# First attention: the high and low parts of Q and K made from PSUM by one ScalarE and one VectorE instruction, and copied to their rows by DMA

## The chip, the cores and the metric

The kernel runs on one core of a Trainium2 chip. The metric is the device time in microseconds of one execution; before the change it is 2598.87 us (median of three runs).

## The reference

The kernel computes one block of a hybrid network on x of 2048 x 128 in fp32:

```
x = x + attn_a(layernorm(x))   # 16 heads of 64, biases, a scale per head, softmax over all 2048 keys,
                               # output projection, residual and a layernorm inside
x = x + ffn(layernorm(x))      # 128 -> 512 -> 128, relu
x = x + attn_b(layernorm(x))   # 8 heads of 128, rotary embedding, causal
x = x + ffn(layernorm(x))

attn_a:  Q = x Wq' + bq,  K = x Wk' + bk,  V = x Wv' + bv
         scores = Q K' * (64 ** -0.5 * adaptive_scale[head]);  softmax;  times V;  times Wo
```

Only the first attention (attn_a) is touched.

## The kernel before, in words

**Precision by parts.** A score needs more precision than one fast product gives. So each operand is split into a high part (rounded to the fp32r format) and a low part (what the rounding left). For a head, four arrays of 128 rows hold Q and K, transposed, with 2048 columns: KH has K-high in both halves of its rows, QL has Q-low in one half and Q-high in the other, QH has Q-high in its upper half (and the rows of maxima in its first rows), KL has K-low there. A score tile is then two products of 128 rows each: KH by QL (L1297) and KL by QH (L1298). There are two sets of the four arrays, for the head in work and the next.

**Pattern.** A unit is one head and one block of 512 queries; a head has four units, a loop turn of the program two heads, so eight units, here numbered 0 to 7. A unit has eight steps of 256 keys. In a step TensorE makes four score products (L1297, L1298) and, with a lag of two steps, sixteen products of probabilities by V (L1247, L1248). ScalarE takes two exponentials of the scores, 128 x 1024 each, to fp32 (L634) and to fp16 (L636). GpSimd subtracts one from the other to get the low part of the probabilities (L449). All engines are programmed apart and meet by semaphores.

**The ring.** Everything else that TensorE does for later units goes through two PSUM banks used in turn, RING: a product is put into one, VectorE takes it out, in order, and the counter `ring_taken` says so. `ring_items_a` writes the order out by hand: sixteen rough score tiles, from which VectorE takes maxima (L855), spread over steps 0 to 6 of a unit; in units 5, 6, 7 and 0 "turned" in step 3 and "output" in step 4 (the output projection of the pair of heads); in steps 3 and 7 of units 0, 1, 4 and 5 one projection each, which makes a block of 512 columns of Q and K for the next head (L1173); in units 2 and 6 the values; and last in step 7 "rows", the transposed maxima (L858 to L860, L1200, L867), which VectorE writes into QH. At step 0 of a unit TensorE waits until all items of the ring are taken.

**A projected block.** VectorE adds the bias and multiplies by the scale, from PSUM into F (L824), Q in rows 0 to 63 and K in rows 64 to 127. ScalarE then copies it in five pieces of 64 rows, rounded, to KH, QL, KH, QL and QH (L594); `PIECES` spreads these over the four steps that follow, one or two in each behind the step's exponentials. Two steps later VectorE subtracts for K-low (L831), GpSimd for Q-low (L426). The first maximum of a head waits for all of it. SP's queue issues only the loads of weights ahead of the attention and what follows it.

In the head of the program the weights are transposed by TensorE and taken from PSUM by ScalarE and VectorE in turn; the four blocks of head 0 are projected there one after another. VectorE does the statistics of each finished unit in step 2 of the next (L888 to L892).

Of the kernel before, what the change touches and what calls it, by code (L numbers as in the profile page):

```python
# [41 lines left out]
P = 128  # L42
# [19 lines left out]
PIECES = ((0, 1), (2,), (3,), (4,))  # L62

WV_AT = 2 * DA + 2
# [121 lines left out]
def build(nc, x, adaptive_scale, Wq, bq, Wk, bk, Wv, bv, Wo, bo, gamma, beta,  # L186
          w_aq, w_ak, w_av, w_ao, W1, b1, W2, b2, rope_cos, rope_sin, out):
    ctx = ExitStack()
    with ctx:
# [18 lines left out]
        F = sb("F", [P, 2, BLK])  # L208
        WST = sb("WST", [P, 2, 3 * DB])
        OSUM = sb("OSUM", [P, 2, BT // 2, DA])  # L210
# [38 lines left out]
        sraw = F[0:DA, 1, P:P + HA]  # L249
# [52 lines left out]
        k_low = sem("k_low")  # L302
# [45 lines left out]
        def _(sp):  # L348
# [7 lines left out]
            sp.dma_start(sraw, adaptive_scale.partition_broadcast(DA)).then_inc(w_in, 16)  # L356
# [14 lines left out]
            sp.dma_start(WVB, w_av).then_inc(bweights, 16)  # L371

# [12 lines left out]
        def _(pool):  # L385
# [31 lines left out]
            pool.wait_ge(wt_act, 5)  # L417
# [34 lines left out]
            for blk in range(BLOCKS):  # L452
                q_low(0, blk, blk)
# [12 lines left out]
            def turn_a(it, first=False, last=False):  # L466
                for ul in range(UNITS_A):
# [5 lines left out]
                    for step in range(STEPS_A):  # L473
                        two, three = (after_a(ul, step, d, first, last) for d in (2, 3))
                        if two and two[0] == "project":
                            q_low(1 - hs, two[1], head * BLOCKS + two[1])
                        elif two:
                            values_rest(1 - hs, two[1], head * 2 + two[1])
# [72 lines left out]
        def _(act):  # L551
# [17 lines left out]
            for i in range(0, 9, 2):  # L569
# [3 lines left out]
                if i < 4:  # L573
                    ins = act.activation(WQK[:, i * 4:i * 4 + 4, 0:P], src4, ACT.Copy)
                elif i < 6:
                    ins = act.activation(WQK[:, 0:8, WV_AT:BV_AT], bank.rearrange("p (a c) -> p a c", c=DA), ACT.Copy)
                elif i < 8:
                    ins = act.activation(WoT[:, (i - 6) * 4:(i - 6) * 4 + 4, :], src4, ACT.Copy)
                else:
                    ins = act.activation(WQK[:, :, P], bank[:, 0:HA], ACT.Copy)  # L580
                ins.then_inc(wt_act, 1)
# [26 lines left out]
            for blk in range(BLOCKS):  # L608
                high_parts_a(0, blk, blk, 0, range(5))
# [15 lines left out]
            def exps_a(it, first=False, last=False):  # L625
                k = SKIP if first else 0
                numbers = {}
                for ul in range(UNITS_A):
                    hs, qb = divmod(ul, BLOCKS)
                    for step in range(STEPS_A):  # L630
# [8 lines left out]
                        for delay, pieces in enumerate(PIECES, 1):  # L639
                            item = after_a(ul, step, delay, first, last)  # L640
                            if item and item[0] == "project":
                                high_parts_a(1 - hs, item[1], LEAD_A - SKIP + it * RING_A + numbers[item],
                                             (head - 1) * BLOCKS * STEPS_A, pieces)
                            elif item and delay == 1:
                                values_first(1 - hs, item[1], LEAD_A - SKIP + it * RING_A + numbers[item])
                            elif item and delay == 2:
                                values_second(1 - hs, item[1], head * 2 + item[1])
                        for item in ring_items_a(ul, step, first, last):
                            numbers[item] = k
                            k += 1  # L650
# [105 lines left out]
        def _(dve):  # L756
# [45 lines left out]
            for i in range(1, 8, 2):  # L802
                dve.wait_ge(wt_put, i + 1)
                bank = QUARTER[i % 4]
                src4 = bank.rearrange("p (a c) -> p a c", c=P)
                if i < 4:
                    ins = dve.tensor_copy(WQK[:, i * 4:i * 4 + 4, 0:P], src4)
                elif i < 6:
                    ins = dve.tensor_copy(WQK[:, 8:HA, WV_AT:BV_AT], bank.rearrange("p (a c) -> p a c", c=DA))
                else:  # L810
                    ins = dve.tensor_copy(WoT[:, (i - 6) * 4:(i - 6) * 4 + 4, :], src4)
                ins.then_inc(wt_dve, 1)
            dve.wait_ge(w_in, 80)

            dve.memset(WQK[DA:P, :, P + 1], 1.0)
            dve.tensor_scalar(WQK[0:DA, :, P + 1], sraw, SCALE_A, None, ALU.mult).then_inc(wt_dve, 1)
# [745 lines left out]
```

## Time and profile before

| | |
|---|---|
| three runs, us | 2598.98, 2596.69, 2598.87 |
| median | 2598.87 |
| profiled execution, first to last instruction (its span) | 2594.6 |
| its TensorE clock, mean granted share | 0.975 |
| busy, share of the span | TensorE 92%, VectorE 68%, ScalarE 67%, GpSimd 57% |
| first attention, first to last score product of its loop | 54.7 to about 1720 us |

A share of busy time is a mean over the whole program. Of the execution with the profile the page gives only the span; the runs' own times are those of the first line, and the part outside the span is the difference of the two.

### The profile page before, as it was taken

To read this page: it belongs to the slowest core of one execution; us is meant where nothing else is said; L and a number is where in the kernel's file an instruction comes from. 1 tells how busy PE (TensorE), PEld (TensorE's weight loads), DVE (VectorE), ACT (ScalarE), POOL (GpSimd) and SP (SyncE) were. 2 spreads that over 40 slices of the span, in tenths; PEclk is the share of its full clock that TensorE was granted. 3 is DMA by queue.
4 is the path that set the end of the run, shared out by engine and by line. 5 is a ranking of instruction groups with operands and counts; after the bars stand their busy time and mean duration, and the time that the engine had idled before them with its cause. 6 is when DMAs were issued, how large, how long until landed. Compare 5 with 4: busy or idle time off the path is not lost.

```text
span 2594.6 us, 47816 instructions
## 1 busy us (share of the span) xinstructions
PE 2390.6 (92%) x17315; PEld 1882.8 (73%) x17315; DVE 1769.3 (68%) x3012; ACT 1732.4 (67%) x2190; POOL 1469.7 (57%) x826
## 2 busy tenths in 40 slices
PE   5999999999899899989989999977899999999998
PEld 3777777677777677767767777754788887888786
DVE  6777767677677677767776777666666665666652
ACT  4877877778688687777878878752455454455554
POOL 5787777677687677767777777753122112122200
PEclk7999999999999999999999999988899999999999
DMA  3000000000000000000000000010000000000000
GB/s 94 1 1 1 1 1 1 2 1 1 2 1 1 2 1 1 2 2 1 1 2 1 1 1 1 1 41 1 1 1 1 1 1 2 1 1 1 1 1 17
DMA packets 15276, 13.06 MB, mean 5 GB/s; under 512 B 3120, under 2 KB 14384, under 8 KB 14768
## 3 DMA queue, kind: packets, MB, share of 16 engines
q1 hardware_dynamic: 15024, 9.72, 1.4%
q8 instruction: 156, 2.56, 0.4%
q14 instruction: 96, 0.79, 0.1%
HBM read 8.67 MB, written 1.05 MB: 4 GB/s over the span
## 4 chain that ended last, share of the span: by engine, by line
PE 46%; issue 26%; DVE 13%; POOL 9%; ACT 4%; SPq 0%; DMA 0%; DVEq 0%; POOLq 0%; ACTq 0%
PE OO L1247 6%; PE RING L1193 6%; PE ST L1297 5%; POOL PAB L449 5%; PE ST L1298 5%; DVE maxes L855 4%; PE OO L1248 4%; PE OO L1436 3%; DVE OSUM L889 2%; PE RING L1214 2%; POOL F L512 2%; PE RING L1173 2%; PE RING L1389 1%; PE ST L1459 1%; ACT PAB L636 1%
## 5 line engine op out<-in xcount | busy, mean ns | idle before, releaser
L449 POOL TENSOR_TENSOR PAB<-PR,PAB 128x1024 f16<-128x1024 f32 x512 | 1093.2, 2137 | 407.8 <-ACT PAB L636 390.1
L855 DVE TENSOR_REDUCE maxes<-RING 128x1 f32<-128x512 f32 (+1 forms) x1344 | 883.9, 670 | 417.4 <-PE RING L1193 294.1
L634 ACT ACTIVATE PR<-ST,lift 128x1024 f32<-128x1024 f32 x512 | 569.1, 1111 | 360.0 <-PE ST L1298 354.0
L1247 PE MATMUL OO<-VP,PAB 128*128 128x194 bf16 x4096 | 688.3, 250 | 5.5 <-POOL PAB L449 2.0
L1248 PE MATMUL OO<-VP,PAB 128*128 128x130 bf16 x4096 | 653.3, 220 | 0.0
L636 ACT ACTIVATE PAB<-ST,lift 128x1024 f16<-128x1024 f32 x512 | 565.8, 1105 | 0.0
L1247 PEld LDWEIGHTS OO<-VP,PAB 128*128 128x128 f16 x4096 | 400.7, 98 | 190.4 <-issue 127.1
L1193 PE MATMUL RING<-KH,QL 128*128 128x512 f32 x1024 | 457.0, 453 | 46.4 <-DVE maxes L855 39.7
L1297 PE MATMUL ST<-QL,KH 128*128 128x512 f32 x1024 | 453.9, 443 | 29.2 <-issue 13.7
L1248 PEld LDWEIGHTS OO<-VP,PAB 128*128 128x128 f16 x4096 | 403.7, 99 | 10.8 <-issue 9.9
L1298 PE MATMUL ST<-QH,KL 128*128 128x512 f32 x1024 | 405.6, 396 | 0.0
L512 POOL TENSOR_TENSOR F<-F,PR 128x512 f32<-128x512 f32 x64 | 81.4, 1272 | 508.9 <-DVE PR L1023 508.9
L719 ACT ACTIVATE PR<-ST 128x512 f32<-128x512 f32 (+1 forms) x320 | 169.4, 529 | 260.5 <-PE ST L1463 258.5
L1193 PEld LDWEIGHTS RING<-KH,QL 128*128 128x128 f32 x1024 | 196.1, 192 | 139.0 <-DVE maxes L855 117.8
L1436 PEld LDWEIGHTS OO<-PAB,PR 128*128 128x128 f32 x1536 | 227.4, 192 | 41.1 <-issue 22.7
L1436 PE MATMUL OO<-PAB,PR 128*128 128x129 f32 x1536 | 250.7, 280 | 0.0
L1297 PEld LDWEIGHTS ST<-QL,KH 128*128 128x128 f32 x1024 | 195.5, 191 | 66.4 <-issue 38.7
L1298 PEld LDWEIGHTS ST<-QH,KL 128*128 128x128 f32 x1024 | 195.9, 191 | 33.0 <-issue 7.2
L700 ACT ACTIVATE ST<-VF 128x512 f32<-128x512 f32 (+1 forms) x320 | 172.0, 538 | 26.7 <-PE ST L1425 15.3
L1459 PE MATMUL ST<-QH,KH 128*128 128x512 f32 (+1 forms) x320 | 146.3, 457 | 1.0
L1389 PE MATMUL RING<-KH,QH 128*128 128x512 f32 (+2 forms) x320 | 129.3, 408 | 14.7 <-ACT PR L719 8.1
L831 DVE TENSOR_TENSOR KL<-F,KH 64x512 fp32r<-64x512 f32 x64 | 120.5, 1882 | 24.5 <-ACT KH L594 24.0
(132 smaller groups left out, 3044.4 us busy)
## 6 DMA issues: line engine op xcount, KB each, us to landing
X<-in_L_attn_a_x SPq DMA_DIRECT2D x4, 256.0 KB, 4.3
SHARED<-in_rope_cos SPq DMA_DIRECT2D x1, 1024.0 KB, 4.9
SHARED<-in_rope_sin SPq DMA_DIRECT2D x1, 1024.0 KB, 7.1
out<-X SPq DMA_DIRECT2D x4, 256.0 KB, 2.3
RAW<-in_L_attn_a_Wq SPq DMA_DIRECT2D x1, 512.0 KB, 7.5
RAW<-in_L_attn_a_Wk SPq DMA_DIRECT2D x1, 512.0 KB, 7.8
RAW<-in_L_attn_a_Wv SPq DMA_DIRECT2D x1, 512.0 KB, 5.7
RAW<-in_L_attn_a_Wo SPq DMA_DIRECT2D x1, 512.0 KB, 6.8
```

What stands on the lines that cost most here:

```text
L449: pool.tensor_tensor(PB[:, s, :], PR[:, step % 2, :], PA[:, s, :], ALU.subtract).then_inc(p_low_pool, 1)
L634: act.activation(PR[:, step % 2, :], ST[step % 2][:, :], ACT.Exp, bias=lift[:, :])
L636: act.activation(PA[:, step % SLOTS_A, :], ST[step % 2][:, :], ACT.Exp, bias=lift[:, :]).then_inc(sa.exps, 1)
L700: act.activation(SB[parity][:, c0:BLK], MB[:, slot, c0:BLK], ACT.Copy).then_inc(sbb.filled, 1)
L855: dve.reduce_max(maxes[:, qt, c:c + 1], bank[:, 0:width], X_AXIS).then_inc(s.ring_taken, 1)
L1193: pe.matmul(bank[:, :], QL[hs][:, at:at + P], KH[hs][:, c * BLK:(c + 1) * BLK], start=True, stop=True).then_inc(sa.ring_put, 1)
L1247: pe.matmul(o, high, v, start=(m == 0 and qt % 2 == 0), stop=False, skip_group_check=True)
L1248: ins = pe.matmul(o[:, 0:V3_AT], low, v[:, 0:V3_AT], start=False, stop=(m == TILES - 1), skip_group_check=True)
L1297: pe.matmul(tile, KH[hs][:, keys], QL[hs][:, q], start=True, stop=False)
L1298: ins = pe.matmul(tile, KL[hs][:, keys], QH[hs][:, q], start=False, stop=True)
L1436: ins = pe.matmul(bank[:, at:at + VB], PRB[:, step % 2, qt * P:(qt + 1) * P], VBS[:, ul // BLOCKS, step, :], start=(step == 0 and qt in (0 ...
L1459: pe.matmul(tile, KH[hs][:, keys], QH[hs][:, q], start=False, stop=False, skip_group_check=True)
```

## The change

The scale is multiplied into the weights and the bias of Q once, in the head of the program. A projected block is then read from PSUM twice: by ScalarE, which adds the bias and rounds, into a new buffer HS (the high parts of Q and K), and by VectorE, which adds the bias and subtracts HS, into F (the low parts). Both use all 128 rows. ScalarE's instruction stands in the step of the projection, behind its exponentials. The bank counts as taken when VectorE is done. SP waits for that and issues six DMAs of 64 rows x 512, which put the parts in their rows of KH, QL, QH and KL. The five pieces, K-low and Q-low go. HS and F are written again only when the moves of two blocks earlier have landed. The weights of Q and K are now all taken from PSUM by VectorE, with the scale; those of V and of the output by ScalarE. The staged weights are one column narrower.

```diff
-PIECES = ((0, 1), (2,), (3,), (4,))
+MOVES = 6
-WV_AT = 2 * DA + 2
+WV_AT = 2 * DA + 1
...
+            def move_parts(hs, blk, item, scores_before):
+
+                sp.wait_ge(sa.ring_taken, item + 1)
+                wait(sp, sa.scores, scores_before)
+                q = slice(blk * BLK, (blk + 1) * BLK)
+                high, low = HS[:, blk % 2, :], F[:, blk % 2, :]
+                for dst, src in ((KH[hs][0:DA, q], high[DA:P, :]), (KH[hs][DA:P, q], high[DA:P, :]),
+                                 (QL[hs][0:DA, q], high[0:DA, :]), (QL[hs][DA:P, q], low[0:DA, :]),
+                                 (QH[hs][DA:P, q], high[0:DA, :]), (KL[hs][DA:P, q], low[DA:P, :])):
+                    sp.dma_start(dst.bitcast(F32), src).then_inc(parts_moved[blk % 2], 16)
...
-            def q_low(hs, blk, index):
-
-                pool.wait_ge(sa.high_ready, index * 5 + 2)
-                at = QL[hs][0:DA, blk * BLK:(blk + 1) * BLK]
-                pool.tensor_tensor(at, F[0:DA, blk % 2, :], at.bitcast(F32), ALU.subtract
-                                   ).then_inc(sa.operands_ready, 1)
...
-            def high_parts_a(hs, blk, item, scores_before, pieces):
-
-                act.wait_ge(sa.ring_taken, item + 1)
-                wait(act, sa.scores, scores_before)
-                q = slice(blk * BLK, (blk + 1) * BLK)
-                f = F[:, blk % 2, :]
-                places = ((KH[hs], DA, DA), (QL[hs], 0, 0), (KH[hs], 0, DA), (QL[hs], DA, 0), (QH[hs], DA, 0))
-                for i in pieces:
-                    dst, to, at = places[i]
-                    act.activation(dst[to:to + DA, q], f[at:at + DA, :], ACT.Copy).then_inc(sa.high_ready, 1)
+            def high_parts_a(hs, blk, bank, item, batch):
+
+                act.wait_ge(sa.ring_put, item + 1)
+                wait(act, parts_moved[blk % 2], batch * MOVES * 16)
+                act.activation(HS[:, blk % 2, :].bitcast(F32R), bank[:, :], ACT.Identity,
+                               bias=WST[:, hs, P:P + 1]).then_inc(sa.high_ready, 1)
...
                         for item in ring_items_a(ul, step, first, last):
+                            if item[0] == "project":
+                                high_parts_a(1 - hs, item[1], RING[(LEAD_A - SKIP + k) % 2],
+                                             LEAD_A - SKIP + it * RING_A + k, head * (BLOCKS // 2) + item[1] // 2)
                             numbers[item] = k
                             k += 1
...
-            def take_projected_a(hs, blk, bank, item, index):
-
-                dve.wait_ge(sa.ring_put, item + 1)
-                wait(dve, sa.operands_ready, index - 1)
-                wait(dve, sa.high_ready, (index - 1) * 5)
-                wait(dve, k_low, index - 1)
-                dve.tensor_scalar(F[:, blk % 2, :], bank[:, :], WST[:, hs, P:P + 1],
-                                  WST[:, hs, P + 1:P + 2], ALU.add, ALU.mult).then_inc(sa.ring_taken, 1)
-
-            def take_k_low(hs, blk, index):
-
-                dve.wait_ge(sa.high_ready, index * 5 + 1)
-                q = slice(blk * BLK, (blk + 1) * BLK)
-                dve.tensor_tensor(KL[hs][DA:P, q], F[DA:P, blk % 2, :], KH[hs][DA:P, q].bitcast(F32),
-                                  ALU.subtract).then_inc(k_low, 1)
+            def take_projected_a(hs, blk, bank, item, index, batch):
+
+                dve.wait_ge(sa.high_ready, index + 1)
+                wait(dve, parts_moved[blk % 2], batch * MOVES * 16)
+                dve.scalar_tensor_tensor(F[:, blk % 2, :].bitcast(F32R), bank[:, :], WST[:, hs, P:P + 1],
+                                         HS[:, blk % 2, :], ALU.add, ALU.subtract).then_inc(sa.ring_taken, 1)
...
             def max_a(hs, qb, i, bank, item, head):
                 if i == 0 and qb == 0:
-                    pe.wait_ge(sa.operands_ready, (head + 1) * BLOCKS)
-                    pe.wait_ge(k_low, (head + 1) * BLOCKS)
-                    pe.wait_ge(sa.high_ready, (head + 1) * BLOCKS * 5)
+                    for moved in parts_moved:
+                        pe.wait_ge(moved, (head + 1) * (BLOCKS // 2) * MOVES * 16)
```

## Rows read from the trace of the kernel before

**Rows 1.** The page, part 1: busy us, share, instructions of each engine.

```profile
PE 2390.6 (92%) x17315; PEld 1882.8 (73%) x17315; DVE 1769.3 (68%) x3012; ACT 1732.4 (67%) x2190; POOL 1469.7 (57%) x826
```

**Rows 2.** Windows of units 0, 1, 4, 5, two without projection, and steps 3 to 4.

```profile
core 0: us, PE busy (x) PEld busy (x) DVE busy (x) ACT busy (x) POOL busy (x), PEclk, DMA share, GB/s
258.06:283.96 25.90, 24.85 (x196) 19.04 (x194) 19.20 (x30) 20.51 (x22) 19.70 (x11) 1.00 0.01 2
283.96:309.78 25.82, 24.48 (x182) 17.67 (x182) 19.73 (x29) 23.04 (x27) 20.39 (x10) 1.00 0.01 2
360.42:385.29 24.87, 23.58 (x184) 17.68 (x182) 18.37 (x28) 19.33 (x20) 18.34 (x10) 1.00 0.01 2
385.29:412.03 26.74, 25.71 (x193) 19.02 (x194) 20.48 (x31) 23.09 (x27) 20.39 (x10) 1.00 0.00 1
1633.02:1654.64 21.62, 21.48 (x180) 16.94 (x178) 14.90 (x25) 16.95 (x18) 17.09 (x9) 1.00 0.00 1
1654.64:1678.03 23.39, 22.79 (x192) 18.14 (x190) 16.29 (x27) 16.95 (x18) 17.12 (x9) 1.00 0.01 2
368.50:375.71 7.21, 6.66 (x50) 4.68 (x48) 5.73 (x9) 4.31 (x5) 4.61 (x3) 1.00 0.00 0
1641.12:1647.06 5.94, 5.80 (x49) 4.38 (x46) 4.96 (x8) 4.31 (x5) 4.63 (x3) 1.00 0.01 3
```

**Rows 3.** Timeline, steps 5 and 6 of the unit at 360.42: start, us.

```profile
376.43 0.63 ACT L594 ACTIVATE KH<-F 64x512 fp32r<-64x512 f32 x1
...
377.09 2.08 DVE L831 TENSOR_TENSOR KL<-F,KH 64x512 fp32r<-64x512 f32 x1 [1.03 <-ACT KH L594]
...
379.95 0.50 PE L1193 MATMUL RING<-KH,QL 128*128 128x512 f32 x1 [0.41 <-DVE maxes L855]
```

**Rows 4.** Groups by line: busy us, mean ns, idle before.

```profile
L831 DVE TENSOR_TENSOR KL<-F,KH 64x512 fp32r<-64x512 f32 x64 | 120.5, 1882 | 24.5 <-ACT KH L594 24.0
...
L892 DVE TENSOR_TENSOR SHARED<-OSUM,rden 128x256 f32<-128x256 f32 x64 | 96.8, 1513 | 2.2
```

**Rows 5.** Groups by line, the operations nearest to the new ones.

```profile
L878 DVE TENSOR_TENSOR XN<-XN,RING 128x512 f32<-128x512 f32 x32 | 22.0, 687 | 28.2 <-PE RING L1214 28.2
...
L663 ACT ACTIVATE PAB<-ST,b1c 128x512 f32<-128x512 f32 x16 | 10.7, 693 | 9.0 <-PE ST L1332 8.8
```

**Rows 6.** Timeline, GpSimd and VectorE in step 7 of unit 3.

```profile
357.02 2.13 POOL L449 TENSOR_TENSOR PAB<-PR,PAB 128x1024 f16<-128x1024 f32 x1 [0.51 <-ACT PAB L636]
...
357.05 2.11 DVE L860 TENSOR_TENSOR negparts<-negmax,negparts 128x4 f32<-128x4 f32 x1
```

**Rows 7.** Timeline of unit 4: step 0's exponential, then step 7.

```profile
361.63 1.12 ACT L634 ACTIVATE PR<-ST,lift 128x1024 f32<-128x1024 f32 x1 [2.03 <-PE ST L1298]
...
381.70 0.47 PE L1297 MATMUL ST<-QL,KH 128*128 128x512 f32 x1
...
383.18 1.11 ACT L634 ACTIVATE PR<-ST,lift 128x1024 f32<-128x1024 f32 x1
...
383.77 0.81 DVE L824 TENSOR_SCALAR F<-RING,WST 128x512 f32<-128x512 f32 x1 [1.12 <-PE RING L1173]
...
384.19 1.11 ACT L636 ACTIVATE PAB<-ST,lift 128x1024 f16<-128x1024 f32 x1
...
384.50 0.67 DVE L867 TENSOR_TENSOR QH<-RING,rowmask 8x512 fp32r<-8x512 f32 x1
```

**Rows 8.** DMA issues of the page: count, KB each, us to landing.

```profile
out<-X SPq DMA_DIRECT2D x4, 256.0 KB, 2.3
```

**Rows 9.** Timeline of the prologue: first maximum's product, GpSimd's last addition.

```profile
37.68 1.19 PE L1193 MATMUL RING<-KH,QL 128*128 128x512 f32 x2 [1.77 <-ACT QH L594]
...
48.53 4.49 POOL L463 TENSOR_TENSOR X<-X,beta_b 128x2048 f32<-128x2048 f32 x1
```

**Rows 10.** Windows: a held subtraction (unit 3), then the turn of the loop.

```profile
355.00:359.30 4.30, 2.52 (x23) 1.85 (x21) 3.83 (x5) 3.76 (x4) 3.63 (x2) 1.00 0.00 0
...
465.60:469.10 3.50, 1.00 (x15) 0.80 (x12) 0.60 (x1) 0.00 (x0) 2.46 (x2) 0.99 0.03 9
469.10:472.50 3.40, 3.34 (x14) 2.50 (x14) 0.69 (x1) 1.23 (x2) 0.00 (x0) 0.50 0.03 7
```

More of the change, by code:

```diff
@@ L301, in build @@
         ones_set = sem("ones_set")
-        k_low = sem("k_low")
+        parts_moved = [sem(f"parts_moved{i}") for i in range(2)]
         p_low_pool = sem("p_low_pool")
@@ L371, in _, with moves_a @@
             sp.dma_start(WVB, w_av).then_inc(bweights, 16)
+            def move_parts(hs, blk, item, scores_before):
[7 more added lines that the diff above has]
+                    sp.dma_start(dst.bitcast(F32), src).then_inc(parts_moved[blk % 2], 16)
+            def moves_a(it, first=False, last=False):
+                k = SKIP if first else 0
+                for ul in range(UNITS_A):
+                    hs = ul // BLOCKS
+                    head = it * 2 + hs + 1
+                    for step in range(STEPS_A):
+                        for item in ring_items_a(ul, step, first, last):
+                            if item[0] == "project":
+                                move_parts(1 - hs, item[1], LEAD_A - SKIP + it * RING_A + k,
+                                           (head - 1) * BLOCKS * STEPS_A)
+                            k += 1
+            for blk in range(BLOCKS):
+                move_parts(0, blk, blk, 0)
+            moves_a(0, first=True)
+            with sp.Fori(1, ITER_A - 1) as it:
+                moves_a(it)
+            moves_a(ITER_A - 1, last=True)
             wait(sp, sa.ring_taken, END_A)
@@ L474, in turn_a @@
                         two, three = (after_a(ul, step, d, first, last) for d in (2, 3))
-                        if two and two[0] == "project":
-                            q_low(1 - hs, two[1], head * BLOCKS + two[1])
-                        elif two:
+                        if two and two[0] == "values":
                             values_rest(1 - hs, two[1], head * 2 + two[1])
@@ L568, in _ @@
                 deviations(b)
-            for i in range(0, 9, 2):
+            for i in range(4, 8):
                 act.wait_ge(wt_put, i + 1)
@@ L638, in exps_a @@
                         head = it * 2 + hs + 1
-                        for delay, pieces in enumerate(PIECES, 1):
+                        for delay in (1, 2):
                             item = after_a(ul, step, delay, first, last)
[L641 to L644, printed above, removed]
+                            if item and item[0] == "values" and delay == 1:
                                 values_first(1 - hs, item[1], LEAD_A - SKIP + it * RING_A + numbers[item])
-                            elif item and delay == 2:
+                            elif item and item[0] == "values":
                                 values_second(1 - hs, item[1], head * 2 + item[1])
                         for item in ring_items_a(ul, step, first, last):
+                            if item[0] == "project":
+                                high_parts_a(1 - hs, item[1], RING[(LEAD_A - SKIP + k) % 2],
+                                             LEAD_A - SKIP + it * RING_A + k, head * (BLOCKS // 2) + item[1] // 2)
                             numbers[item] = k
@@ L801, in _ @@
             dve.tensor_copy(later_keys_t[:, :], mask_raw[:, 1, :]).then_inc(const_r, 1)
-            for i in range(1, 8, 2):
+            dve.memset(score_scale[:, :, 1], 1.0)
+            dve.wait_ge(w_in, 80)
+            link(dve.tensor_scalar(score_scale[:, :, 0], sraw, SCALE_A, None, ALU.mult))
+            for i in range(4):
                 dve.wait_ge(wt_put, i + 1)
[L804 to L812, printed above, removed]
@@ L921, in body_a @@
                             normalise_a((ul - 1) % UNITS_A, u)
-                        two = after_a(ul, step, 2, first, last)
-                        if two and two[0] == "project":
-                            take_k_low(1 - hs, two[1], index + two[1])
                         late = (step - 1) % STEPS_A in LOW_BY_DVE and not (first and ul == 0 and step == 0)
@@ L1149, in _ @@
                     pe.wait_ge(vw_in, 48)
[L1150 to L1151 removed]
+                if 4 <= i < 8:
+                    pe.wait_ge(wt_dve, i - 3)
+                elif i == 8:
+                    pe.wait_ge(wt_act, 1)
                 bank = QUARTER[i % 4]
```

46 lines of the change are left out of this document (22 added, 24 removed).

## The prediction

> **What bounds the kernel now.** I read the page first: TensorE is busy 92% of the span, VectorE, ScalarE and GpSimd between 57 and 68% [rows 1]. So TensorE sets the pace and work taken from another engine is worth only the TensorE waits that it causes. These can't be read from busy shares. The first attention repeats one pattern, so next I cut it into units (one head's block of 512 queries, eight steps) and compared their lengths in the windows view, each from the first score matmul of a unit (L1297) to that of the next [rows 2]. The reader is to see how regular they are. A unit without a projection takes 21.62 us; with "turned" and "output" in it 23.39. The same two kinds with two projected blocks (at steps 3 and 7) take 24.87 and 26.74. Steps 3 and 4 together grow from 5.94 to 7.21 us when a projection is put into them; its matmuls are fp32 and no wait stands in that stretch that the other lacks, so 1.27 us is what a projection costs TensorE itself. The change can't give that back. What it can give back is the rest.
>
> Third, the timeline of one unit and the edge to the next, to find that rest, and with it what a projection at step 7 is followed by.
>
> **What the stalls around a projection are worth.** With N = base + 2 x 1.27, by unit of the pair of heads (numbered 0 to 7, projections in 0, 1, 4, 5) [rows 2]:
> - unit 0: 23.39 + 2.54 = 25.93, takes 25.90: nothing to gain
> - unit 1: 21.62 + 2.54 = 24.16, takes 25.82: 1.66 to gain
> - unit 4: 24.16, takes 24.87: 0.71
> - unit 5: 25.93, takes 26.74: 0.81
>
> Where it comes from: ScalarE's first copy releases the K-low subtraction on VectorE, which takes 2.08 us and makes the maxima late, so that TensorE waits at 379.95 [rows 3]. This instruction takes 1.88 us in the mean [rows 4] for 64 x 512, where a VectorE operation that reads PSUM and one SBUF tensor takes 0.69 for 128 x 512 [rows 5]. The reason stands in another pair of rows: GpSimd's subtraction runs from 357.02 to 359.15, and VectorE's 128 x 4 subtraction that starts at 357.05 lasts 2.11 us, to the moment at which the other ends [rows 6]. VectorE instructions with two SBUF tensors are held by GpSimd. Of the two stalls, that after a step-3 project is unit 4's 0.71 (its predecessor has no projection); that after a step-7 project falls into the next unit and is unit 5's 0.81. So units 2 and 6, which follow such units, hold 0.81 each as well.
>
> The new version has no such subtraction: high and low are made by one ScalarE and one VectorE instruction. All of this is saved: eight iterations of unit 1 (13.3) and 2 (6.5), seven of units 4, 5 and 6 (5.0, 5.7, 5.7; the last head has no successor): **36 us saved**. The removed ScalarE pieces (five of 64 x 512 per block, 0.63 each by the KH row of [rows 3]: 3.15) and GpSimd's Q-low are worth no more than that: TensorE never waits for them otherwise.
>
> **What the change adds at step 7.** Today VectorE takes the projected block straight from PSUM. Then it takes the rows of maxima, and the first score matmul of the next unit waits for that. Step 7 begins at 381.70, F starts at 383.77, QH at 384.50 and lasts 0.67, and the next unit begins at 385.29 [rows 7, 2]: 3.59 us, of which TensorE fills all but 0.3. After the change VectorE waits for ScalarE's high part first, and ScalarE has this instruction in its queue behind both exponentials of the same step. Queued behind the waiting VectorE instruction is the rows instruction, and for that TensorE waits. From the start of step 7:
> - first exponential at +1.21, as ScalarE is free (the unit that starts at 360.42 has it at 361.63 [rows 2, 7])
> - second one 1.01 later, lasting 1.11: +3.33 [rows 7]
> - Identity with a bias, 128 x 512 from PSUM: 0.69, by the Relu with a bias of this shape [rows 5]; bounds 0.55 (half of the exponential's 1.11) and 0.75. With 0.02 ahead of it: +4.04
> - hand-over to VectorE 0.03 (376.43 + 0.63 against 377.09 [rows 3]): +4.07
> - low part: the rows instruction starts 0.73 after it, as after F today [rows 7]; bounds 0.6 and, if GpSimd holds it, see below: +4.80
> - rows 0.67, then 0.12 to the matmul (384.50 + 0.67 against 385.29 [rows 7, 2]): **+5.59 instead of +3.59**
>
> 2.0 us per step-7 projection. There are two per head for 15 heads, 30 in all: **60 us lost**. This is time with TensorE idle, and nothing behind it is waiting to catch up, for TensorE is the engine that is behind. Bounds with ScalarE and VectorE at their lower ends: 1.75 each, 52 us.
>
> **At step 3** the projection comes last on TensorE, ScalarE's exponentials have just ended, so Identity starts at once, but the block is taken 0.7 us later than now (0.69 + 0.03). The second maximum of step 4 needs that bank; today it is put with about 0.35 us in hand, so 0.35 are left as a wait: 30 x 0.35 = **10 us lost** (bounds 0 and 21).
>
> **The moves.** Six DMAs of 128 KB per block on SP's queue, which has nothing else to do in the loop. For a DMA the nearest row is the output's: 256 KB land in 2.3 us [rows 8]. Three of these for 768 KB are 7 us, six in turn 14. The first reader of the last block comes one unit after it, and the buffer of a block is written again one unit later: 24.9 us or more [rows 2]. Hidden, at any of these prices. The Trainium skill ("DMA: Bandwidth & Descriptors", Rules for kernel authors) speaks against moving partition halves by separate transfers: they share the same engines, and one transfer over all partitions is better. No run here shows it yet; if it made every block three times as long in the queue it would still be hidden in the loop.
>
> **The prologue** has no such cover. There the blocks follow each other closely, blocks 2 and 3 wait for the moves of 0 and 1, and the first maximum, now at 37.68, waits for all [rows 9]. At 3 to 4 us a block I get to 41 to 44 us. Part of it is covered: the GpSimd addition that ends at 53.02 [rows 9] holds VectorE until then anyway. Weights by VectorE alone cost up to 1. I take **3 us lost**, bounds 0 and 16 (7 us a block).
>
> **Sum.** The profiled execution spans 2594.6, the median of the runs is 2598.87, so 4.3 us lie outside the span. 2598.9 + 60 + 10 + 3 - 36 = 2636 us, 1.4% slower.
>
> **Rivals.** (1) The clock falls in the new gaps. Between heads TensorE did 1.00 us of work in 3.50, and in the next 3.4 us it is granted 0.50, which is 1.2 GHz [rows 10]. The new gap, about 2 us, is shorter than that one and follows full work; the stretch with the held subtraction of [rows 6], in which TensorE works 2.52 of 4.30 us, kept its clock at 1.00 [rows 10]. If it fell at each of the 30 edges, the next 3.4 us, at half rate, would do the work of 1.7 in full, so the unit is about 1.5 us longer: 2681. At a third of them: 2651. The Trainium skill ("TensorE: Matmul & The Clock Gate", Why this matters for your kernels) warns of idle gaps between bursts for just this. (2) GpSimd holds the new VectorE instruction. It would start at +4.07, while GpSimd's subtraction runs from about +3.4 to +5.5, so it would end about 1.35 later: 40 us more, 2676. For it: it has an SBUF tensor and two scalars per partition from SBUF at most; against: the addition that reads XN and a PSUM bank has 687 ns in the mean of 32 [rows 5], none held. The Trainium skill ("SBUF — State Buffer", Who interferes with whom) says that only two SBUF tensors collide; by that, this rival is out. (3) On the other side, no slower: the holding goes away in other places. The 30 ns between 357.02 and 357.05 [rows 6] decide 2 us at units 3 and 7, fourteen times (27 us), and the normalisation L892 takes 1.51 in the mean [rows 4], 0.7 of which I read as held, in 64 units (45 us). If the idle edges shift GpSimd against VectorE so that both are free, 72 us go: 2564. It decides from 37 us on, half of it. Against: without projections these units run the same instructions in the same rhythm as before. The 30 ns alone: 2609. (4) The edge of step 7 costs less than I count and it is faster: the point is 0.77 us per edge instead of 2.0 ((36 - 10 - 3) / 30), and the two exponentials alone are 2.1 long. I see no way.
>
> **Chances.** Forecast 66%, its own range 2618 to 2652 (edge 1.75 to 2.1, step 3 0 to 0.7, prologue to 16, not all at one end); the 30 ns race alone with it 8%; clock 12%; held instruction 5%; holding gone, or something unseen that makes it no slower 9%. Range 2608 to 2668. What this kernel's measurement can tell from no change is 0.2%, 5 us. Faster 0.06, within 0.03, slower 0.91.
>
> **What would show it.** After: Identity directly behind the second exponential of step 7 (mean 0.55 to 0.7), the low part directly behind it (0.7 to 0.8), the first L1297 of units 1, 2, 5, 6 idle for about 2 us with VectorE's rows as releaser; the step-7-to-unit edge 5.6 us. Units 0, 1, 4, 5 at 28.3, 26.5, 26.5, 28.3, units 2 and 6 0.8 shorter, 3 and 7 as they are. L831 and L426 are gone, ScalarE's busy time falls by some 160 us and this does nothing. I am wrong if step 7 isn't longer, if a clock of 0.5 shows at the edges, or if units 3 and 7 change.

## The result, and the profile after

| | before | after |
|---|---|---|
| runs, us | 2598.45 median of 4 (2596.69 to 2598.98) | 2645.07 median of 4 (2644.73 to 2649.16) |
| ratio after / before | | 1.0186 [1.0172, 1.0201] |
| span of the profiled execution | 2594.6 | 2642.9 |

The median rose by 46.6 us (1.8%; the ratio in the table is 1.9%); forecast were 37 us (2636), range 2608 to 2668. The page of after, part 1, against [rows 1]:

```profile
PE 2379.4 (90%) x17315; PEld 1889.0 (71%) x17315; DVE 1712.3 (65%) x2950; ACT 1577.8 (60%) x1933; POOL 1364.8 (52%) x762
```

ScalarE has 155 us less to do, GpSimd 105, VectorE 57, and TensorE as many matmuls as before. TensorE's own busy time fell by 11.2 us while the span grew by 48.3, so it must be waiting longer. So I cut both traces at the first score product of each step (the line is L1296 now) and took differences of lengths. Five units of after in the windows view, numbered 0, 1, 4, 5 and 7:

```profile
core 0: us, PE busy (x) PEld busy (x) DVE busy (x) ACT busy (x) POOL busy (x), PEclk, DMA share, GB/s
266.19:294.19 28.00, 25.24 (x197) 19.03 (x194) 19.48 (x29) 19.32 (x20) 20.08 (x11) 1.00 0.13 30
294.19:320.44 26.25, 23.70 (x182) 17.67 (x182) 18.10 (x27) 18.21 (x18) 17.07 (x9) 1.00 0.27 61
370.18:396.43 26.25, 23.70 (x185) 17.65 (x182) 18.11 (x27) 18.21 (x18) 18.68 (x10) 1.00 0.14 32
396.43:424.36 27.93, 25.27 (x194) 19.05 (x194) 19.39 (x29) 18.21 (x18) 17.08 (x9) 1.00 0.25 57
452.30:483.64 31.34, 23.11 (x190) 18.16 (x190) 18.48 (x27) 17.98 (x18) 20.48 (x12) 0.94 0.01 3
```

Units 0, 1, 4 and 5 were forecast at 28.3, 26.5, 26.5 and 28.3. Unit 2 went from 26.90 us to 25.99, unit 6 from 28.85 to 27.95, unit 3 stayed at 23.75. Unit 7, in which the change has nothing, went from 28.27 to 31.3. The timeline of unit 4's step 7 and the edge behind it, to be read against [rows 7] (start, us):

```profile
391.03 0.48 PE L1296 MATMUL ST<-QL,KH 128*128 128x512 f32 x1
...
391.82 2.12 DVE L863 TENSOR_TENSOR negparts<-negmax,negparts 128x4 f32<-128x4 f32 x1
...
392.03 1.02 PE L1173 MATMUL RING<-XNT,WST 128*128 128x512 f32 x2
...
393.25 1.11 ACT L650 ACTIVATE PAB<-ST,lift 128x1024 f16<-128x1024 f32 x1
...
394.24 0.69 ACT L607 ACTIVATE HS<-RING,WST 128x512 fp32r<-128x512 f32 x1
...
394.43 2.12 POOL L474 TENSOR_TENSOR PAB<-PR,PAB 128x1024 f16<-128x1024 f32 x1 [0.51 <-ACT PAB L650]
...
394.96 0.75 DVE L834 SCALAR_TENSOR_TENSOR F<-RING,WST,HS 128x512 fp32r<-128x512 f32 x1 [1.02 <-ACT HS L607]
...
395.63 0.67 DVE L870 TENSOR_TENSOR QH<-RING,rowmask 8x512 fp32r<-8x512 f32 x1
...
396.43 0.49 PE L1296 MATMUL ST<-QL,KH 128*128 128x512 f32 x1 [1.59 <-DVE QH L870]
```

The chain is the one forecast: the last exponential, Identity behind it at +3.21, the low part at +3.93, the rows at +4.60, the next unit at +5.40. The 4-element subtraction L863 is held here too, but ends at +2.91, before the chain needs it. ScalarE starts Identity 0.99 us after it started the second exponential, as it spaces the two exponentials.

Summed over the trace, after minus before:

| stretch | forecast | measured |
|---|---|---|
| step 7 with a projection (3.60 to 5.40, 30 times) | +60 | +54.5 |
| step 4 | +10 | +6.7 |
| stalls saved (step 2 -38.0, step 6 -10.8, less +10.2 in step 3) | -36 | -38.6 |
| prologue, to the first score product | +3 | +5.1 |
| step 0, a clock of 0.5 behind six edges, 1.6 us each | rival 1 | +9.7 |
| step 7 of unit 7, the turn of the loop, five times | 0 | +15.4 |
| after the first attention (here the last step of its loop belongs to this part) | 0 | -4.6 |
| sum | +37 | +48.2 of 48.3 |

By unit, the stalls saved are 13.0, 7.2, 5.0, 6.3 and 6.4 us in units 1, 2, 4, 5 and 6, forecast 13.3, 6.5, 5.0, 5.7 and 5.7. Step 3 of units 1, 2, 5 and 6 became 0.35 us longer each time: TensorE waits 0.52 us there for VectorE's maxima, where it waited 0.20. Ahead of these maxima on VectorE stands the normalisation (L892 before, L895 now), which took 1513 ns in the mean and now takes 1809:

```profile
L895 DVE TENSOR_TENSOR SHARED<-OSUM,rden 128x256 f32<-128x256 f32 x64 | 115.8, 1809 | 2.2
```

That this is what makes the maxima late is read from the order of the instructions; no run tried it.

The part after the first attention, in the windows view, before and then after. The same 4981 instructions keep TensorE busy for 4.3 us less, and the trace has it at the lower clock for 68.3 us instead of 78.5:

```profile
1718.32:2594.60 876.28, 795.44 (x4981) 662.43 (x4978) 539.34 (x1107) 415.01 (x771) 178.56 (x152) 0.96 0.02 5
```

```profile
1771.17:2642.90 871.73, 791.10 (x4981) 658.61 (x4978) 539.48 (x1107) 415.02 (x771) 178.61 (x152) 0.96 0.02 5
```

One of the six falls of the clock, against a stretch at an edge that kept it, in the windows view (391.03 to 396.43 is the step 7 shown above):

```profile
391.03:396.43 5.40, 3.42 (x27) 2.27 (x24) 4.15 (x6) 3.38 (x4) 4.39 (x3) 1.00 0.01 3
...
643.20:646.60 3.40, 3.31 (x14) 2.43 (x14) 0.69 (x1) 1.64 (x2) 0.21 (x1) 0.59 0.75 174
```

Of 30 such edges, in which TensorE is busy 3.26 to 3.44 of 5.40 us, six are followed by 3.4 us at the lower of its two levels (1.2 GHz); all six lie behind unit 1 or 5. The window shown begins a little ahead of the fall, hence 0.59.

### The profile page after: what moved, and what is told of

It is laid out like the page before. It is cut to its first block, busy times and chain, and to the rows that moved or that the text cites. A ratio compares the mean times of both kernels' runs of the same rounds, so it can differ in the third digit from the quotient of the medians.

```text
span 2642.9 us, 47576 instructions
## 1 busy us (share of the span) xinstructions
PE 2379.4 (90%) x17315; PEld 1889.0 (71%) x17315; DVE 1712.3 (65%) x2950; ACT 1577.8 (60%) x1933; POOL 1364.8 (52%) x762
## 4 chain that ended last, share of the span: by engine, by line
PE 56%; issue 20%; DVE 15%; POOL 6%; ACT 3%; DVEq 0%; DMA 0%; SPq 0%; POOLq 0%; ACTq 0%
PE RING L1192 9%; PE OO L1246 9%; PE ST L1296 7%; PE ST L1297 6%; PE OO L1247 6%; DVE maxes L858 4%; PE OO L1435 3%; POOL PAB L474 3%; DVE OSUM L892 2%; POOL F L533 2%; PE RING L1213 2%; PE RING L1181 2%; DVE negparts L863 2%; PE RING L1388 1%; PE ST L1458 1%
## 5 line engine op out<-in xcount | busy, mean ns | idle before, releaser
L1296 PE MATMUL ST<-QL,KH 128*128 128x512 f32 x1024 | 455.4, 445 | 86.3 <-DVE QH L870 57.2
L1192 PE MATMUL RING<-KH,QL 128*128 128x512 f32 x1024 | 448.7, 450 | 42.7 <-DVE maxes L858 36.7
L1247 PEld LDWEIGHTS OO<-VP,PAB 128*128 128x128 f16 x4096 | 406.1, 99 | 10.8 <-issue 9.9
L1296 PEld LDWEIGHTS ST<-QL,KH 128*128 128x128 f32 x1024 | 195.9, 191 | 124.4 <-issue 87.4
L1435 PE MATMUL ST<-PAB,PR 128*128 128x129 f32 x640 | 124.6, 277 | 2.4 <-ACT PR L733 2.4
```

The lines of the kernel that those rows point to most:

```text
L1192: pe.matmul(bank[:, :], QL[hs][:, at:at + P], KH[hs][:, c * BLK:(c + 1) * BLK], start=True, stop=True).then_inc(sa.ring_put, 1)
L1247: ins = pe.matmul(o[:, 0:V3_AT], low, v[:, 0:V3_AT], start=False, stop=(m == TILES - 1), skip_group_check=True)
L1296: pe.matmul(tile, KH[hs][:, keys], QL[hs][:, q], start=True, stop=False)
L1435: ins = pe.matmul(bank[:, at:at + VB], PRB[:, step % 2, qt * P:(qt + 1) * P], VBS[:, ul // BLOCKS, step, :], start=(step == 0 and qt in (0 ...
```

## The experiments

Each run was timed in turns with the kernel before, and its ratio is to that.

**1. The second projection of a pair in step 6 instead of 7**, in the kernel after. The second half of the values of units 2 and 6 moves to step 6 with it. If the wait at the edge is the cause, it must shrink when Identity no longer stands behind the exponentials of step 7 with TensorE waiting.

```diff
-HEAD_STEPS = (3, 7)
+HEAD_STEPS = (3, 6)
```

> The changed kernel with the second projection (and the second half of the values) of a unit in step 6 in place of step 7. Theory: the loss is the chain exponentials, high part, low part, rows at the unit's edge, so with a step between projection and edge it goes: steps 6 and 7 of units 0, 1, 4, 5 together take 8.05 us now, and then 6.3 (3.9 + 2.35) if VectorE's small subtraction runs free, 7.1 if GpSimd holds it and the rows come late; 30 times, and the clock falls behind the edges (some 10 us) go too. So 2580 to 2607, I take 2600. Rival: the loss comes from the moves or from the new instructions as such: the place doesn't matter, 2635 to 2655.

Measured: 2596.68 (2593.45 to 2599.75), ratio 0.9991 [0.9982, 1.0000]. Step 7 behind a projection is 3.75 instead of 5.40 (-55.6 in all); steps 6 are 42.9 longer, as they hold the projection or the values now, the other steps 7 29.8 shorter; no edge lets the clock fall (-9.7). One digit in the order of work is worth 48.7 us of span, all that the change had cost. What ends the edge now, in the timeline:

```profile
377.96 2.13 POOL L474 TENSOR_TENSOR PAB<-PR,PAB 128x1024 f16<-128x1024 f32 x1 [0.52 <-ACT PAB L650]
377.98 2.12 DVE L863 TENSOR_TENSOR negparts<-negmax,negparts 128x4 f32<-128x4 f32 x1
378.33 0.69 ACT L607 ACTIVATE HS<-RING,WST 128x512 fp32r<-128x512 f32 x1 [0.45 <-PE RING L1173]
...
380.03 0.74 DVE L834 SCALAR_TENSOR_TENSOR F<-RING,WST,HS 128x512 fp32r<-128x512 f32 x1
380.16 0.27 PE L1199 MATMUL RING<-ident,negparts 128*8 128x128 f32 x1 [0.94 <-DVE negparts L863]
...
381.49 0.49 PE L1296 MATMUL ST<-QL,KH 128*128 128x512 f32 x1
```

Identity starts as soon as the projection ends. The low part has no idle time in front of it: VectorE is in L863, which GpSimd holds for 2.12 us. TensorE waits 0.94 us for it ahead of the transposed maxima and then has its own products up to the next unit. This had been hidden under the longer chain.

**2. Three waits ahead of the loop on TensorE's queue**, in the kernel after. They are met at once and only move the code that follows. It asks whether unit 7's 3 us come from the place of the code or from the new moves.

```diff
+            for _ in range(3):
+                pe.wait_ge(consts, 4)
```

> The changed kernel with three more TensorE waits (on a semaphore long reached) ahead of the first loop. The turn of the loop has become 3.1 us longer, five times, with TensorE waiting for nothing that the profile shows. Theory: the three waits that the change took out of TensorE's program ahead of the loop moved the loop's first instruction within the blocks in which code is loaded; put back, the last step of unit 7 goes from 9.9 to about 6.9 us and the time from 2645 to about 2630. Rival: the new loop on SP's queue or the moves make the turn longer: 2645, last step 9.9.

Measured: 2633.00 (2630.50 to 2635.35), ratio 1.0127 [1.0112, 1.0143]. The turn is back at 6.85 to 7.22 us (-15.7 in all), while nine edges instead of six lose the clock (+4.6). The score product behind a turn, in before, after and this run, from three timelines:

```profile
469.16 0.79 PE L1297 MATMUL ST<-QL,KH 128*128 128x512 f32 x1 [2.56 <-issue]
```

```profile
483.64 0.80 PE L1296 MATMUL ST<-QL,KH 128*128 128x512 f32 x1 [5.61 <-issue]
```

```profile
483.89 0.79 PE L1296 MATMUL ST<-QL,KH 128*128 128x512 f32 x1 [2.50 <-issue]
```

The releaser "issue" says that no engine was waited for. With the same moves and the same arithmetic the wait is 3.1 us shorter, so the moves alone don't cause it.

**3. Identity between the two exponentials of step 7**, in the kernel after. The first chain says that the place in ScalarE's queue is what costs: one exponential less in front is worth the spacing of two, 1.0 us per edge.

```diff
+                        early = [i for i in ring_items_a(ul, step, first, last) if i[0] == "project" and step == 7]
+                        if early:
+                            high_parts_a(1 - hs, early[0][1], RING[(LEAD_A - SKIP + k) % 2],
+                                         LEAD_A - SKIP + it * RING_A + k,
+                                         (it * 2 + hs + 1) * (BLOCKS // 2) + early[0][1] // 2)
...
-                            if item[0] == "project":
+                            if item[0] == "project" and not early:
```

> The changed kernel with ScalarE's high part of a step-7 projection between the two exponentials of that step, not behind both. Theory (a chain with each term in line): the edge falls from 5.40 to 1.21 + 1.03 + 0.69 + 0.03 + 0.67 + 0.67 + 0.12 = 4.4 us, 30 times, so 29 us less and with fewer clock falls up to 39 less: 2606 to 2616. Rival: the edge is set by something else, as the subtraction held by GpSimd to +2.9 and TensorE's own work: less than 10 us of gain, 2635 to 2645.

Measured: 2609.66 (2605.08 to 2611.20), ratio 1.0036 [1.0022, 1.0049]. Step 7 is 4.40 us (-30.1 in all), no edge lets the clock fall (-9.5). ScalarE in the timeline of one such step:

```profile
385.18 1.11 ACT L648 ACTIVATE PR<-ST,lift 128x1024 f32<-128x1024 f32 x1 [0.52 <-PE ST L1302]
386.19 0.68 ACT L607 ACTIVATE HS<-RING,WST 128x512 fp32r<-128x512 f32 x1
386.76 1.11 ACT L655 ACTIVATE PAB<-ST,lift 128x1024 f16<-128x1024 f32 x1
```

A shift of 1.01 us in ScalarE's queue shortens TensorE's edge by 1.00.

**4. The same edit as 1, in the kernel before.** Is the earlier place good by itself?

> The kernel before, with nothing but the second projection moved from step 7 to 6. It tells how much of the first run's gain is the place alone. The edge costs little there (3.59 us, TensorE at work for nearly all of it), and K-low still stalls TensorE two steps after each projection: 2590 to 2605. If it gains as much as the changed kernel does, the place is worth it by itself and the change nothing.

Measured: 2615.73 (2613.75 to 2621.27), ratio 1.0062 [1.0048, 1.0075]: slower than before, where 2590 to 2605 was expected. Step 0 of units 1, 2, 5 and 6 went from 2.98 to 4.98 us (+61.0 in all). The timeline of one:

```profile
289.87 2.13 POOL L449 TENSOR_TENSOR PAB<-PR,PAB 128x1024 f16<-128x1024 f32 x1 [1.20 <-ACT PAB L636]
...
290.47 0.63 ACT L594 ACTIVATE QL<-F 64x512 fp32r<-64x512 f32 x1
...
291.13 1.42 DVE L831 TENSOR_TENSOR KL<-F,KH 64x512 fp32r<-64x512 f32 x1 [2.67 <-ACT QL L594]
...
292.58 1.29 DVE L855 TENSOR_REDUCE maxes<-RING 128x1 f32<-128x512 f32 x2
...
293.32 0.50 PE L1193 MATMUL RING<-KH,QL 128*128 128x512 f32 x1 [1.82 <-DVE maxes L855]
```

One step earlier, the K-low subtraction lands in step 0 ahead of that step's maxima; it waits for ScalarE's pieces behind step 7's exponentials (VectorE idle 2.67), then the maxima come late and TensorE idles 1.82. Steps 0 and 1 of these units pay 76.7 us for this; step 2, where the stall was before, gets 38.3 back, steps 6 and 7 together 18.5, and step 3 costs 4.2. Part of the 76.7 is the clock: ten times it falls to its lower level in step 0 or 1 behind such a wait, at 1.6 us each about 16 us (an estimate with the price found in the kernel after). The edges of this kernel are only 2.5 us long. So the good place is good only with the new scheme, which has no K-low.

**5. Head 0's moves shared by two queues**, three issued by ScalarE and three by SP, in the kernel after. The prologue's 5.1 us against SP's issuing.

```diff
+                for dst, src in ((KH[0][0:DA, q], high[DA:P, :]), (KH[0][DA:P, q], high[DA:P, :]),
+                                 (QL[0][0:DA, q], high[0:DA, :])):
+                    act.dma_start(dst.bitcast(F32), src).then_inc(parts_moved[blk % 2], 16)
...
-                move_parts(0, blk, blk, 0)
+                move_parts(0, blk, blk, 0, range(3, 6))
```

> The changed kernel with the moves of head 0 shared: ScalarE issues the two K-high copies and one of Q-high, SP the other three. SP takes 0.64 us to issue one, so 24 of them take 15.4 us in a row. Theory: the prologue's loss (first score product of the loop at 59.8 against 54.7 us) is this issuing; halved, the first maximum comes at about 38.5 in place of 45 and the loop starts at 54 to 55: 2640. Rival: the loss is the weights taken by VectorE alone, or the landing of the transfers: 2645, the loop still at 59 or later.

Measured: 2648.03 (2643.54 to 2653.89), ratio 1.0184 [1.0170, 1.0198]: no gain. The first product for a maximum starts at 42.35 instead of 44.70 us, 2.3 us earlier, where 38.5 was expected, and the loop starts 2.3 earlier, at 57.5 instead of the 54 to 55 expected. Even that is uncertain: the same product starts at 43.98 to 45.31 in the five kernels here with one queue and six moves, and at 42.35, 43.66 and 42.91 in the three with two (runs 5, 7 and 8), 1.7 apart in the mean. Ten edges lost the clock in place of six (+6.4 at step 0), and the part after the first attention took 4.1 more, with 10.2 us more at the lower clock; this ate the gain. The prologue's chain in the kernel after, from its timeline:

```profile
38.93 1.24 SPq L384 DMA_DIRECT2D KH<-HS  x2
40.21 0.60 SPq L384 DMA_DIRECT2D QL<-HS  x1
40.86 0.60 SPq L384 DMA_DIRECT2D QL<-F  x1
41.49 0.60 SPq L384 DMA_DIRECT2D QH<-HS  x1
42.13 0.60 SPq L384 DMA_DIRECT2D KL<-F  x1
...
44.70 1.19 PE L1192 MATMUL RING<-KH,QL 128*128 128x512 f32 x2 [2.61 <-DMA KL<-F]
```

SP issues a move every 0.64 us, 24 of them without a pause from 27.48 to 42.73.

**6. Twelve moves per block.** The kernel after, with six extra transfers of 64 x 128 per block into rows that nobody reads. It asks whether the moves cost anything in the loop.

```diff
-MOVES = 6
+MOVES = 12
...
+                for i in range(6):
+                    rows, at = slice(i % 2 * DA, (i % 2 + 1) * DA), slice(i // 2 * P, (i // 2 + 1) * P)
+                    sp.dma_start(SPARE[rows, blk % 2, at], (high, low)[i % 2][rows, at]
+                                 ).then_inc(parts_moved[blk % 2], 16)
```

> The changed kernel with six more transfers per block (64 x 128 each, to rows that nobody reads), waited for like the others. Theory: in the loop the moves are hidden (12 x 0.64 = 7.7 us of issuing, with 12 us or more between projections and a whole unit until the first reader), so the steps stay as they are; in the prologue 24 more issues are 15 us more: 2655 to 2662. Rival: the transfers disturb the engines or the loading of code in the loop: steps get longer, 2670 and more.

Measured: 2663.69 (2661.03 to 2667.99), ratio 1.0256 [1.0241, 1.0272]. The prologue is 13.64 us longer, the steps of the loop, summed by their number (0 to 7) over the whole loop, within 0.7 us of what they were, the part after the first attention 3.9 longer, again with 10.2 us more at the lower clock. The first product for a maximum:

```profile
58.32 1.19 PE L1197 MATMUL RING<-KH,QL 128*128 128x512 f32 x2 [10.37 <-DMA SPARE<-F]
```

Its 13.62 us over 44.70 are for 24 more issues: 0.57 each, for 32 KB as for 128 KB nearly the same. It is the number of transfers that counts there, and in the loop not even that. The Trainium skill ("DMA: Bandwidth & Descriptors", Rules for kernel authors) speaks against moving partition halves by separate transfers, because they share the same engines. What this run shows is a price of issuing; no run here moved a block by one transfer, so the page's reason was not tried.

**7. Step 6, two queues and the three waits together.**

> The changed kernel with projections in steps 3 and 6, the moves of head 0 on two queues, and three more TensorE waits ahead of the loop. If the three causes add up: 2597 - 15 (turn of the loop) - 5 (prologue) = 2577, faster than the kernel before by 0.8%. If they overlap, 2580 to 2597.

Measured: 2574.75 (2574.52 to 2580.10), ratio 0.9916 [0.9902, 0.9929]. Against run 1 the span is 21.3 us shorter: 13.8 at the turn of the loop, 3.8 in the step behind it, 3.4 after the first attention (6.8 us less at the lower clock), 0.2 in the prologue. So the two queues gave nothing here.

**8. Run 7 without the held subtraction.** The low part of the maxima is 128 x 4, from two SBUF tensors. Four instructions of one column take the second operand as a scalar per partition.

```diff
-                    dve.tensor_tensor(negparts[:, BT:AUX], negmax[:, :], negparts[:, 0:BT],
-                                      ALU.subtract).then_inc(s.max_ready, 1)
+                    for i in range(BT):
+                        ins = dve.tensor_scalar(negparts[:, BT + i:BT + i + 1], negmax[:, i:i + 1],
+                                                negparts[:, i:i + 1], None, ALU.subtract)
+                    ins.then_inc(s.max_ready, 1)
```

> The kernel of the run before this one, with the low part of the maxima made by four VectorE instructions on one column each (one SBUF tensor and a scalar per partition) in place of one on two SBUF tensors. That one is held by GpSimd for 2.1 us in 49 of 64 units. Theory: only two SBUF tensors are held, so the four run free in some 0.4 us: units 3 and 7 lose 1.8 us each in the loop, units 0, 1, 4, 5 some 0.65, unit 6 some 0.7: 45 us less, 2525 to 2540. Rival: a VectorE instruction that reads SBUF at all is held, or the wait moves on to something else: 2570 to 2580.

Measured: 2532.34 (2531.74 to 2536.45), ratio 0.9747 [0.9734, 0.9761]: 2.5% faster than the kernel before, the best version here. A step 7 of it in the timeline, with GpSimd at work:

```profile
350.67 2.13 POOL L475 TENSOR_TENSOR PAB<-PR,PAB 128x1024 f16<-128x1024 f32 x1 [0.49 <-ACT PAB L656]
...
350.70 0.58 DVE L870 TENSOR_SCALAR negparts<-negmax,negparts 128x1 f32<-128x1 f32 x4
...
351.33 0.27 PE L1207 MATMUL RING<-ident,negparts 128*8 128x128 f32 x1 [0.24 <-DVE negparts L870]
```

Four instructions in 0.58 us, beginning 30 ns after GpSimd's subtraction, where one in the same position took 2.12 in run 1. By groups, the kernel after and this one:

```profile
L863 DVE TENSOR_TENSOR negparts<-negmax,negparts 128x4 f32<-128x4 f32 x96 | 106.1, 1105 | 3.3
```

```profile
L870 DVE TENSOR_SCALAR negparts<-negmax,negparts 128x1 f32<-128x1 f32 x384 | 55.4, 206 | 3.4
```

Against run 7, step 7 of units 0, 1, 4 and 5 gained 22.3 us, the other steps 7 with the loop's turn 22.4, steps 3 7.0; what follows the first attention took 12.9 more. This part isn't the same in both: the second attention makes its maxima in the same function, and 32 of the 96 subtractions stand there. The windows view of this part, run 7 and then run 8, has 96 more VectorE instructions:

```profile
1701.03:2572.80 871.77, 791.10 (x4981) 658.55 (x4978) 539.40 (x1107) 415.02 (x771) 178.56 (x152) 0.96 0.02 5
```

```profile
1649.96:2534.60 884.64, 797.08 (x4981) 662.86 (x4978) 549.86 (x1203) 415.02 (x771) 178.47 (x152) 0.95 0.02 5
```

Nothing held the subtraction there. By groups over this part, the kernel before and run 9:

```profile
L860 DVE TENSOR_TENSOR negparts<-negmax,negparts 128x4 f32<-128x4 f32 x32 | 5.2, 162 | 1.1
```

```profile
L861 DVE TENSOR_SCALAR negparts<-negmax,negparts 128x1 f32<-128x1 f32 x128 | 18.5, 207 | 1.6 <-DVE negparts L859 0.6
```

So 0.16 us became 0.58, thirty-two times. The Trainium skill ("SBUF — State Buffer", Who interferes with whom) has a VectorE instruction collide with GpSimd when two of its inputs lie in SBUF and GpSimd reads SBUF, or when it runs in a two-port mode. The rows of the loop agree with the first; the prediction, in its rival 2, quoted only that one. No run here shows a two-port mode.

**9. The same four instructions in the kernel before.**

> The kernel before with nothing but the four one-column instructions in place of the held one. Step 7 of units 3 and 7 is 1.5 us shorter in the loop, unit 6 some 0.7: 2570 to 2578. If it reached 2535, the changed kernel's scheme would be worth nothing in the version of the last run.

Measured: 2579.56 (2576.69 to 2580.24), ratio 0.9927 [0.9913, 0.9940]. Step 7 of unit 3 is 2.62 instead of 4.15, of unit 6 4.42 instead of 4.78, the turn 5.57 instead of 7.09 in the mean. It is 1.6 us above the range expected, and the part after the first attention, where the edit was expected to do nothing, is 3.3 longer. Run 8 is 66 us below the kernel before, this run 20: the four instructions alone don't make the former.

**10. The same four in the kernel after.**

> The changed kernel with nothing but the four one-column instructions. At the edges with a projection in step 7 the held subtraction ends at +2.9 us and the chain at +5.4, so it is covered there: the edges stay at 5.4, and only units 3, 6 and 7 gain, as in the kernel before: 2612 to 2622. Rival: the held instruction is part of the edge: 2600 or less.

Measured: 2648.47 (2645.20 to 2652.00), ratio 1.0191 [1.0177, 1.0205], no gain where 2612 to 2622 was expected. Units 3, 6 and 7 gained 18.0 us, and the edges stayed at 5.40 (+0.9 with the last head's steps 7), as expected of a subtraction that is covered there. But twelve edges lost the clock instead of six (+9.3 in steps 0), and 2.1 more went in the step behind the turn, 1.0 in the prologue and 8.1 after the first attention, where the four instructions run too: together +3.4, where the span grew by 3.7.

## Why the prediction was right

The direction, the place and the cause of the loss were right, and so was the range. That the sum came out so near is partly luck. Its four terms measured +27.7 us together, not +37 (54.5 + 6.7 + 5.1 - 38.6), and 20.5 us came from places that it had at nothing (9.7 + 15.4 - 4.6). Of its three signs of being wrong two came: a clock of 0.5 showed at edges, and unit 7 changed.

**The edge of step 7** was right in its mechanism and in nearly all of its size. I had 5.59 us, the trace 5.40; of the 0.19, 0.14 lie ahead of the low part (+4.07 against +3.93: I let Identity start behind the exponential's end, and it started 0.12 before it) and 0.06 in its spacing to the rows (0.73 against 0.67). Run 3 shows the mechanism by a shift within ScalarE's queue, run 1 by a shift of the step.

**The stalls saved** were 38.6 against 36. The comparison of units with and without a projection gave this before any of the new instructions had a price; the held K-low subtraction was the reason given, and units 1, 2, 4, 5 and 6 changed as listed. The net hides two sizes: steps 2 and 6 gave 48.8 us, and step 3 took 10.2 back, behind a normalisation that now takes longer. One reading behind it was wrong: steps 3 and 4 with a projection do hold a wait that the others lack, 0.55 us for VectorE's maxima against 0.14, so of the 1.27 us only 0.86 are TensorE's work. The change left this wait (0.52), so the sum didn't suffer.

**Step 4** 6.7 against 10, **the prologue** 5.1 against 3, both inside their bounds. The prologue's first maximum came at 44.70 instead of the 41 to 44 forecast: per block SP's issuing took 6 x 0.64 = 3.84 us, and the landing 2.3 behind the last. Run 6 shows that the number of transfers is what scales there; run 5 found less to gain by a second queue than issuing alone would give.

**The moves** are hidden in the loop: run 6 doubled their number, and no step, by its number, changed by more than 0.7 us in all.

**The clock, rival 1**, came in part. I gave it all 30 edges or a third of them; it was six, 9.7 us, and which edges it takes differs from kernel to kernel: six in run 6, nine in run 2, ten in run 5, twelve in run 10, none in runs 1, 3, 7, 8 and 9, whose edges are shorter. The forecast had it at nothing. It isn't tied to these edges: run 4 has short ones and ten falls behind the 1.8 us of idle time that it put into step 0. Why one of two equal edges lets the clock fall and the next doesn't stays open.

**Rival 2** is out: the new VectorE instruction takes 751 ns in the mean of 64, and 0.75 in the edge above, inside GpSimd's subtraction (394.43 to 396.55). **Rival 3** didn't come: units 3 and 7 kept their held subtraction, and in the kernel after, L863 takes 1105 ns in the mean where L860 took 618 before. Both means are over 96; of the 64 in the first attention 27 took over 1 us before and 51 after, the 32 in the second never. The shift went the other way: it is held at the edges too, and the normalisation takes longer (1809 ns against 1513). This costs nothing only as long as the longer chain covers it, and when run 1 took that chain away, the holding was what ended the edge.

**What was missing** is the turn of the loop, 15.4 us, the largest error of the sum and the reason why 46.6 came out instead of 37. I had said that unit 7 would not change. Run 2 shows that three instructions which do nothing undo it. The profile has DMA packets of its "instruction" queue in this stretch, so loading of code may be the cause; but the kernel before has them there too, and no run showed them to be what TensorE waits for.

**After the first attention** the differences are -4.6 to +12.9 us. Most is the clock: counting half of the time at the lower level as lost (an estimate from the traces' own record of the clock), this part is 836.3 to 839.1 us long in the nine kernels with the one subtraction. In runs 8, 9 and 10, where the four instructions replace it in the second attention too, it is 843.8 to 844.7, 6.7 to 7.1 longer than in the kernel that each is compared with. Why the clock differs in a part that wasn't changed stays open. A gain or loss of 0.3% in a whole time should not be given to an edit without the lengths of its own steps.

**Outside the span** I counted 4.3 us, from the median of the runs and the span of another execution. Where one execution of this kernel has both on record, the difference is 2.2 to 2.3 us. The sum doesn't use it.

## What to carry to other kernels

Splitting a product between two engines in a row puts the first engine's queue into the chain of the second. The step and the place in the first one's queue decided here between 1.9% slower (behind both exponentials of step 7), 0.4% slower (between them) and no change (in step 6), with the same instructions; so when an operation is handed to another engine, choose its place again. A stall that another covers is not gone: after each repair read again what ends the wait. And try rewriting a tiny instruction on two SBUF tensors that runs beside GpSimd; four instructions with a scalar per partition replaced 2.1 us by 0.6. Where nothing holds the tiny instruction they lose: in the second attention they replaced 0.16 us by 0.58, and that part became some 7 us longer. Used in the first attention alone they should give those 7 us back (an estimate; no run tried it).

## What the runs showed of the hardware

- Turning the program's loop cost TensorE 2.4 to 3.2 us of "issue" or 5.35 to 6.4; three instructions ahead of the loop that do nothing decided it (runs 2 and 7 against after and run 1).
- SP takes 0.64 us to issue one SBUF-to-SBUF transfer of 64 x 512, and 24 in a row take 15.3 us, while each lands in 2.3.
- Identity with a bias, 128 x 512 from PSUM, takes 688 ns in the mean of 64; the low part from PSUM, a bias and an SBUF tensor 751.
- A 5.40-us stretch in which TensorE was busy for 3.3 to 3.4 us kept its clock 24 times and lost it 6 times in the kernel after; the same edges lost it 6 to 12 times in four other kernels.
- A 128 x 4 subtraction of two SBUF tensors took 2.12 us beside a GpSimd subtraction and 0.16 alone; four of 128 x 1 with a scalar per partition took 0.58 in both places.
